# A two-layer recurrence on one core: VectorE's sum of the output moved from in front of layer 0's pair of rests to behind it

## The reference

```python
def layer(x, h0, Wx, Wh, b):
    xW = jnp.einsum('ntd,dh->nth', x, Wx) + b
    def step(h_prev, xw_t):
        h_next = jnp.tanh(h_prev @ Wh + xw_t)
        return (h_next, h_next)
    _, hs = jax.lax.scan(step, h0, jnp.swapaxes(xW, 0, 1))
    return jnp.swapaxes(hs, 0, 1)

x = x + layer(x, cond_1024, L0_cond_Wx, L0_cond_Wh, L0_cond_b)
x = x + layer(x, cond_1024, L1_cond_Wx, L1_cond_Wh, L1_cond_b)
return x
```

## Time and profile before

| | |
|---|---|
| median of 3 runs | 2039.12 us (2035.76 to 2039.52) |
| profiled execution, its own time | 2037.84 us |
| its span in the trace | 2035.8 us |
| granted TensorE clock | 1.00 |
| TensorE (PE) busy | 2020.9 us, 99% |
| VectorE (DVE) busy | 1866.6 us, 92% |
| ScalarE (ACT) busy | 1524.0 us, 75% |
| GpSimd (POOL) busy | 862.2 us, 42% |

### The profile page before, as it was taken

How to read it: one execution, slowest core, us unless ns; L and a number is a source line. 1 busy time by engine, 2 the same in 40 slices (tenths; PEclk the granted TensorE clock), 3 DMA queues, 4 the chain that set the end, 5 groups by cost and what they waited for, 6 DMA issues and landing times.

```text
span 2035.8 us, 251040 instructions
## 1 busy us (share of the span) xinstructions
PE 2020.9 (99%) x110552; PEld 1838.4 (90%) x110552; DVE 1866.6 (92%) x12254; ACT 1524.0 (75%) x7426; POOL 862.2 (42%) x4090
## 2 busy tenths in 40 slices
PE   8999999999999999999999999999999999999999
PEld 6999999999999999999999999999999999999997
DVE  5999999999999999999999999999999999999997
ACT  4777777777777777777777777777777777777776
POOL 5444444444444444444444444444444444444442
PEclk9999999999999999999999999999999999999999
DMA  3000000000100000100000000000001010100000
GB/s 108 24 28 24 28 24 28 24 28 24 28 24 28 24 28 24 28 24 28 24 28 24 28 24 28 24 28 24 28 24 28 24 28 24 28 24 28 24 27 18
DMA packets 112015, 56.75 MB, mean 28 GB/s; under 512 B 12432, under 2 KB 111008, under 8 KB 111520
## 3 DMA queue, kind: packets, MB, share of 16 engines
q1 hardware_dynamic: 111168, 53.53, 9.2%
q10 hardware_dynamic: 576, 1.18, 0.2%
q0 software_dynamic: 32, 0.02, 0.0%
HBM read 37.90 MB, written 16.78 MB: 27 GB/s over the span
## 4 chain that ended last, share of the span: by engine, by line
PE 99%; issue 0%; DVE 0%; DMA 0%; ACT 0%; ACTq 0%
PE ps_rec L295 39%; PE ps_rec L277 37%; PE ps_xw L249 22%; DMA bias<-b_in 0%; ACT h L418 0%; DVE zt L516 0%; PE ps_rec L342 0%; DVE x_mid L553 0%; DVE z L528 0%; ACTq L470 0%; ACT ps_xw L381 0%; DVE x_out L562 0%; ACTq L478 0%
## 5 line engine op out<-in xcount | busy, mean ns | idle before, releaser
L204 POOL TENSOR_TENSOR h<-h 128x8 f32<-128x8 f32 x4064 | 845.3, 208 | 1150.4 <-ACT h L418 991.5
L295 PE MATMUL ps_rec<-wh_part,h 128*32 128x128 bf16 (+1 forms) x60984 | 1172.5, 216 | 0.7 <-issue 0.7
L277 PE MATMUL ps_rec<-wh,h 128*32 128x128 f32 (+1 forms) x33008 | 1129.1, 255 | 8.6 <-ACT h L418 5.0
L418 ACT ACTIVATE h<-z 128x16 f32<-128x16 f32 x4066 | 720.8, 216 | 483.9 <-DVE z L528 356.1
L295 PEld LDWEIGHTS ps_rec<-wh_part,h 128*32 128x32 bf16 x60984 | 915.3, 97 | 112.5 <-issue 0.9
L516 DVE STREAM_TRANSPOSE zt<-ps_rec 128x64 f32<-128x64 f32 x4096 | 778.7, 228 | 76.8 <-PE ps_rec L277 12.6
L407 ACT ACTIVATE ps_rec<-xw,mask 128x128 f32<-128x128 f32 x2040 | 726.9, 356 | 0.9 <-issue 0.6
L277 PEld LDWEIGHTS ps_rec<-wh,h 128*32 128x32 f32 (+1 forms) x33008 | 648.6, 105 | 76.3 <-ACT h L418 14.0
L528 DVE TENSOR_REDUCE z<-zt 128x16 f32<-128x48 f32 x4066 | 664.1, 202 | 2.5 <-DVE zt L516 1.5
L204 DVE TENSOR_TENSOR h<-h 128x16 f32<-128x16 f32 x2034 | 372.7, 183 | 75.3 <-ACT h L418 0.5
L249 PE MATMUL ps_xw<-wx,x_pe 128*32 128x128 f32 x8240 | 320.2, 273 | 1.4 <-ACT ps_xw L381 1.4
(11 more groups left out here) (23 smaller groups left out, 23.6 us busy)
## 6 DMA issues: line engine op xcount, KB each, us to landing
x_pe<-x_t SPq DMA_DIRECT2D x256, 64.0 KB, 1.9
x_dve<-x_t SPq DMA_DIRECT2D x256, 64.0 KB, 2.0
out_t<-x_out SPq DMA_DIRECT2D x256, 64.0 KB, 1.7
wh<-wh_in SPq DMA_DIRECT2D x1, 1024.0 KB, 4.8
wx<-wx_in SPq DMA_DIRECT2D x1, 1024.0 KB, 9.1
wx<-wx_in ACTq DMA_DIRECT2D x1, 512.0 KB, 5.1
wx<-wx_in SPq DMA_DIRECT2D x1, 512.0 KB, 4.8
wh<-wh_in SPq DMA_DIRECT2D x1, 512.0 KB, 7.2
```

The costliest lines, as they stand in the source:

```text
L204: return eng.tensor_tensor(step[:, tiles, to], step[:, tiles, of], h_bits(l, n)[:, tiles, of], ALU.subtract)
L277: mm = pe.matmul(out, state, wh[l][:, k, g * P:(g + 1) * P][:, cols], start=False, stop=k == KC - 1 and is_whole(l, n), skip_group_check=True,
L295: mm = pe.matmul(rows(ps_rec[l][n % 2], g)[:, cols], h_bits(l, n - 1)[:, k, :], wh_part[l][:, i, at:at + P][:, cols], start=False, stop=k ...
L418: act.activation(h_of(l, n)[:, tiles, :], src[:, tiles, :], ACT.Tanh).then_inc(h_count(l, n)[0], 1)
```

## The change

VectorE's slot calls `rests(n0)` first and `sum_out(before)` behind it. Nothing else differs.

```diff
@@ -571,10 +571,10 @@
                     total(0, n0)
                 if s % S4 == 0 and (c := s // S4) < NG:
                     dve.wait_ge(x_dve_loaded[c % 2], DMA * (c // 2 + 1))
+                if n0 is not None:
+                    rests(n0)
                 if before is not None:
                     sum_out(before)
-                if n0 is not None:
-                    rests(n0)
                 if n1 is not None:
                     turn(1, n1)
                     lower(1, n1)
```

## The result

The changed kernel is slower: 2047.39 us (median of 6 runs, 2045.77 to 2049.07) against 2036.77 (6 runs), a ratio of 1.0047 with an interval of 1.0035 to 1.006. The forecast was 2039, no difference that can be measured; the 2039.12 us given for the kernel before were the median of its first 3 runs, and against these 6 the change costs 10.6 us, 0.5%. Its profiled execution has a span of 2045.6 us against 2035.8, 9.8 more.

What follows compares the result with a forecast made beforehand. TensorE was taken to bound the loop at 1.95 us a step. All terms were 0 but for a 1 us allowance, so profiled 2037.84 us plus 1 gave 2039 us, range 2033 to 2053.

Steps and rivals of the forecast that it cites:

- What bounds the kernel: Steady loop: TensorE sets the pace at 1.95 us a step, with VectorE close behind.
- the rings: Each layer's state passes round several engines once a step; layer 1's weight load leads its first matmul by only 0.02 us.
- In front of the first rest: VectorE before layer 0's rests: tanh, not the sum, releases the first rest, so moving the sum gains 0 us.
- Behind the second rest: VectorE before layer 1's transposes: the moved sum still fits, delay 0 to 0.01 us; taken as 0, allowing 1 us.
- slots like B: Some three quarters of steps, where the moved sum leaves 0.00 us spare before layer 1's transposes.
- Its waits: The sum's waits for tanh and x_dve: long fulfilled in either place, the x_dve wait moving to the first rest; 0 us.
- POOL's reads: POOL's SBUF reads lengthen the moved sum and delay layer 1's transposes: 2053 to 2068 us, chance 0.13.
- POOL holds the sum to its own end: The moved sum waits until POOL's rests end, delaying layer 1's transposes: 61 us more, 2099 us, chance 0.04.
- The sum overlaps its neighbours: Rival claimed the opposite: no overlap on VectorE in the new place, 152 us more, 2190 us, chance 0.04.
- the first rest come earlier anywhere: Faster rival: the old sum held up the first rest behind tanh, gain 5 us, 2033 us, chance 0.07.
- the side that had 0.25: Chance given to a measurably slower kernel; same had 0.68 and faster 0.07.
- the forecast's own range: 2036 to 2047 us for the no-change case, from the spread of runs and the 8 us bound on transpose delay.

Runs made afterwards that it cites:

- the sum twice: Changed kernel with the x_dve wait moved behind the rests, plus the output sum made a second time into a spare buffer; 2084.53 us.
- The wait alone: Kernel before, output sum left in front of the rests, x_dve wait moved between the sum and the first rest; 2043.22 us.
- the first variant: Changed kernel with the x_dve wait (every fourth slot) moved behind the rests, in front of the output sum; 2040.27 us.
- the wait on the transposes: Kernel before with the x_dve wait moved to the slot's head, so layer 0's first transpose has two waits in every fourth slot; 2049.95 us.
- the waits exchanged: Changed kernel with the fourth slot's two waits before the first rest reordered, tanh's written first and x_dve's second; 2034.03 us.

## Why the prediction was wrong

**What bounds the kernel: right, and it was the warning.** The loop goes at TensorE's pace and the rings have next to no slack. Layer 0's had about 0.05 us in front of the load behind the rests. Layer 1's had less: with the sum twice its transposes are 0.10 us late in two slots of four and the steps behind lose 0.08 to 0.10, which fits the 0.02 us that the prediction read.

**In front of the first rest: "no gain", right; "0 us", in three slots of four.** There tanh releases the rest in the changed kernel as before, 0.033 us behind. In the fourth slot the rest does not stay where it was but comes 0.076 us later, by the step that failed, below.

**Behind the second rest: right, as long as the rests are on time.** The sum was forecast to start 0.12 us behind the second rest and to let the transposes go on time in slots like B. In the changed kernel it starts 0.12 (in the fourth slot and its predecessor 0.09) behind and the transposes are 0.044 or 0.045 us behind TensorE's last matmul in three slots of four, 0.043 before. The spare room was read to a hundredth, and the variant with the wait behind the rests has the steady step of the kernel before.

**"Its waits": this step failed.** It said that the wait for x_dve "now sits on the first rest instead of on the sum" and priced it at 0, because the transfer lands long before. That is true of the transfer and beside the point. An instruction that waits for two semaphores was two instructions here; the wait written last, tanh's, became one of its own, and the rest came 0.076 us later. The wait alone costs 0.027 us in four steps, 6.9 us in all; the rests so delayed push the sum and with it layer 1's transposes by 0.05 us, another 0.013 to 0.015 us, 3.3 to 3.8 in all; together they make the 10.7 us of the steady loop. The kernel before had the wait for x_dve in front of L562, together with that for tanh and that for the store's buffer, and its trace shows the extra instruction there (L561); its price lay in VectorE's idle time in front of the rests, which I had called free.

**The rivals.** None of them was it. POOL's reads: the sum at 1002.26 begins inside POOL's rests, which run from 1002.11, and takes 0.18 us; the medians by slot are 0.178 to 0.194, so at most 0.016 us, on slots that have the room. That POOL holds the sum to its own end is excluded by the same rows. The Trainium skill ("SBUF — State Buffer", section "SBUF: two separate sides") has the second to start wait for the whole instruction of the first; the measured 0.016 us decides against that for these small instructions. The sum overlaps its neighbours: 1000.34 + 0.19 = 1000.53, and the transposes are at 1000.44. Nor did the first rest come earlier anywhere: its median is 0.033 us behind tanh, 0.032 before.

**The numbers.** 2047.39 lies inside 2033 to 2053, on the side that had 0.25, and 0.4 above the 2036 to 2047 of the forecast's own range. That the range held it was luck: its upper end came from the first rival, POOL's reads, which was not the cause, and the forecast itself had no change where there was a loss of 10.6 us.

## What to carry to other kernels

When the first instruction of a group is moved away, look at which waits stood ahead of it: a wait that stands there in the code falls to whatever is now first. If that one already waits for something late, write the late wait first and the early one behind it, or put the early wait behind that instruction, as the first variant does. Written ahead of a late one, a wait whose condition is long met is not free on a ring that is tight to hundredths of a microsecond.

## What the runs showed of the hardware

- Two semaphores in front of one VectorE instruction: 0.109 us from tanh's end to the rest instead of 0.033, and 0.114 from a matmul's end to the transpose instead of 0.043, if the late one stands last in the code; 0.033 if it stands first (the changed kernel, the wait on the transposes, the waits exchanged). Where both signals are there before VectorE comes, the extra instruction shows no price: one stands in front of nearly every L553 of the kernel before (L552, 1018 of them), and L553 overlaps the reduction before it by 0.082 us, as L562 does.
- A VectorE instruction holds the next up by its length less about 0.08 us: in the changed kernel the sum begins 0.078 us before the end of the second rest, and layer 1's transposes 0.070 before the end of the sum (medians).
- A VectorE instruction that comes too late in one step need not in the next: with the sum made twice, steps of 2.04 and 1.95 us alternate.
